# Graph kernel: opening with neighbour products by quarter of h

## The reference

```
h = relu(layernorm(x))
mask = adj > 0 ; deg = sum(mask, axis=1)
agg = mask @ h / max(deg, 1)
x = x + relu(concat(h @ W_self + b_self, agg @ W_nb + b_nb) @ W_comb + b_comb)

state = relu(layernorm(x))
5 times:
  s_in = state @ in_W.T + in_b ; s_out = state @ out_W.T + out_b
  a_in = adj @ s_in ; a_out = adj.T @ s_out
  r, z = sigmoid([a_in, a_out, state] @ (r_W, z_W).T + (r_b, z_b))
  h_hat = tanh([a_in, a_out, r * state] @ h_W.T + h_b)
  state = (1 - z) * state + z * h_hat
out = x + tanh(state @ o1_W.T + o1_b) @ o2_W.T + o2_b
```

## Time and profile before

| | |
|---|---|
| median of 3 runs | 1261.09 us |
| the profiled execution's own time | 1261.28 us |
| its span | 1259.5 us |
| TensorE busy | 1240.4 us, 98% |
| VectorE, ScalarE, GpSimd busy | 58%, 22%, 0% |
| chain of work that ended last | 88% TensorE |
| first instruction of TensorE | 6.21 us |
| first mask product (mean_sum(0)) | 40.19 us |
| first dense product | 61.16 us |
| mean granted TensorE clock, whole span | 0.995 |

### The profile page before, as it was taken

How to read it: one execution, slowest core, us unless ns; L and a number is a source line. 1 busy time by engine, 2 the same in 40 slices (tenths; PEclk the granted TensorE clock), 3 DMA queues, 4 the chain that set the end, 5 groups by cost and what they waited for, 6 DMA issues and landing times.

```text
span 1259.5 us, 12854 instructions
## 1 busy us (share of the span) xinstructions
PE 1240.4 (98%) x4922; PEld 603.4 (48%) x4922; DVE 725.3 (58%) x1222; ACT 279.8 (22%) x544; POOL 3.0 (0%) x9
## 2 busy tenths in 40 slices
PE   7999999999999999999999999999999999999998
PEld 5666654444444444444444444444444444444445
DVE  5577664055657468258547438845734963672674
ACT  4765311010104012022302103311211330120121
POOL 0000000000000000000000000000000000000000
PEclk9899999999999999999999999999999999999999
DMA  8354084006194920840480381074066019116201
GB/s 305 135 169 167 35 317 175 1 0 266 63 335 179 334 100 1 300 167 0 169 299 0 106 307 56 5 286 178 0 227 240 1 66 348 54 36 232 88 1 67
DMA packets 44410, 182.97 MB, mean 145 GB/s; under 512 B 3521, under 2 KB 13506, under 8 KB 28610
## 3 DMA queue, kind: packets, MB, share of 16 engines
q1 hardware_dynamic: 43344, 178.40, 38.9%
q0 software_dynamic: 720, 3.67, 0.8%
q10 hardware_dynamic: 290, 0.14, 0.0%
HBM read 147.07 MB, written 35.13 MB: 145 GB/s over the span
## 4 chain that ended last, share of the span: by engine, by line
PE 88%; DVE 1%; issue 0%; ACT 0%; DVEq 0%; ACTq 0%
PE bank L308 87%; PE bank L471 1%; PE bank L424 0%; DVE work L1203 0%; DVE ST L1205 0%; DVE H L1053 0%; DVE work L1201 0%; PE bank L377 0%; DVE DR L1021 0%; DVE work L1177 0%; DVE work L1181 0%; DVE AT L1010 0%; DVE LF L1148 0%; DVE res L1413 0%; DVE stat L960 0%
## 5 line engine op out<-in xcount | busy, mean ns | idle before, releaser
L308 PE MATMUL bank<-slot,LF 128*128 128x512 f16 x1792 | 389.4, 379 | 1.3 <-ACT m_buf L738 0.7
L308 PEld LDWEIGHTS bank<-slot,LF 128*128 128x128 f16 x1792 | 175.1, 98 | 212.7 <-issue 2.9
L308 PE MATMUL bank<-X,W 128*128 128x512 f32 x384 | 180.5, 593 | 0.0
L308 PE MATMUL bank<-XT,W 128*128 128x512 f32 x288 | 135.4, 593 | 0.0
L308 PEld LDWEIGHTS bank<-X,W 128*128 128x128 f32 x384 | 72.6, 190 | 87.9 <-issue 86.8
L308 PE MATMUL bank<-A,SN 128*128 (+1 forms) x256 | 97.2, 380 | 0.0
L308 PE MATMUL bank<-work,WG 128*128 128x512 f32 x224 | 97.1, 593 | 0.0
L308 PE MATMUL bank<-AT,SN 128*128 (+1 forms) x256 | 97.1, 379 | 0.0
L308 PEld LDWEIGHTS bank<-XT,W 128*128 128x128 f32 x288 | 54.8, 190 | 68.8 <-issue 68.1
L1224 DVE TENSOR_TENSOR u_buf<-bank,m_buf 128x512 f32<-128x512 f32 x16 | 11.1, 692 | 130.7 <-PE bank L308 130.7
L738 ACT ACTIVATE m_buf<-bank 128x512 f32<-128x512 f32 x40 | 23.8, 596 | 227.9 <-PE bank L308 227.9
(11 more groups left out here) (170 smaller groups left out, 1367.3 us busy)
## 6 DMA issues: line engine op xcount, KB each, us to landing
slot<-quad_d SPq DMA_DIRECT2D x112, 1024.0 KB, 5.6
WG<-in_adj SPq DMA_DIRECT2D x32, 512.0 KB, 4.3
quad_d<-AT SPq DMA_DIRECT2D x14, 1024.0 KB, 5.0
quad_d<-A SPq DMA_DIRECT2D x14, 1024.0 KB, 6.3
SN<-in_x SPq DMA_DIRECT2D x2, 1024.0 KB, 10.3
x_d<-SN POOLq DMA_DIRECT2D x4, 512.0 KB, 2.9
x1o<-x_d SPq DMA_DIRECT2D x1, 2048.0 KB, 8.2
out<-res SPq DMA_DIRECT2D x4, 512.0 KB, 3.0
```

The lines of the kernel that those rows point to most:

```text
L308: return pe.matmul(o, l, r, start=start, stop=stop, skip_group_check=again)
```

## The change

- By quarter: mean_sum(0) waits for quarter 0 of h only, and mean_sum(4), (8) and (12) for the others. On VectorE normal(0), normal(1) and low(0) stand ahead of the loop; low(1) to low(3) stand behind masks at i = 2, 5 and 9 (LOW_AT), normal(2) and normal(3) behind the first two of them. On ScalarE high(0) stands ahead of the loop, high(1) to high(3) at i = 1, 4 and 8 (HIGH_AT).
- The layernorm's factor is multiplied by SCALE once, so h32 holds scaled values without relu. The maximum with zero over each quarter goes; high is now an activation Relu, low takes max(h, 0) minus the high half in its one instruction, and the copies of transposed h apply relu and 1/SCALE.
- turn_h(0) to turn_h(3) move behind mean_sum(5), (7), (9) and (11) (TURN_AT), to banks 6 and 7; their copies stand four tiles later in the orders of ScalarE and VectorE.
- bias0's products and gcol's move behind mean_sum(1) (BIAS_AT). For gcol GpSimd first scales the gate weights by the bias columns (4 operations of 768 columns) and adds them in pairs (2), so that TensorE has 12 products with a column of ones.
- Ten products on zeros (WARM) stand ahead of TensorE's first work, and a small square root ahead of ScalarE's; both wait for two VectorE memsets.
- move_adj(0) goes ahead of the loop's first convert; W12's copies come behind high(0).

```diff
--- before.py
+++ after.py
@@ -37,6 +37,11 @@
 H2_AT = 12
+HIGH_AT = [1, 4, 8]
+LOW_AT = [2, 5, 9]
+TURN_AT = [5, 7, 9, 11]
+BIAS_AT = 1
+WARM = 10
 
@@ -117,6 +122,7 @@
         diag = work[:, 8192:16384].bitcast(FP16).rearrange("p (w t n) -> p w t n", w=2, t=NT)
+        idle16 = work[:, 0:2 * BN].bitcast(FP16)
         xs = SN[:, :, :, :].rearrange("p t s d -> p t (s d)").bitcast(FP32)
@@ -139,6 +145,8 @@
         h32 = AT[:, 1, :, :].rearrange("p t n -> p (t n)").bitcast(FP32).rearrange("p (t d) -> p t d", t=NT)
+        scaled = AT[:, 2, :, :].rearrange("p t n -> p (t n)").bitcast(FP32)[:, 0:4 * GATES].rearrange(
+            "p (w j n) -> p w j n", w=2, j=2)
         fusedS = AT[:, 3, :, :].rearrange("p t n -> p (t n)").bitcast(FP32)[:, 0:4 * GATES].rearrange(
@@ -158,6 +166,8 @@
         setup_done = sem("setup_done")
+        w12_sum, gsum, gcol_out = sem("w12_sum"), sem("gsum"), sem("gcol_out")
+        warm = sem("warm")
         var_ready, sqrt_ready = sem("var_ready"), sem("sqrt_ready")
@@ -294,6 +304,15 @@
         def _(pool):
+            pool.wait_ge(ld_c, 48)
+            for w in range(2):
+                pool.wait_ge(ld_w[w], 32)
+                for j in range(2):
+                    nc.gpsimd.tensor_scalar(scaled[:, w, j, :], wgR[w][:, j, :], col[:, 2 * w + j:2 * w + j + 1], None,
+                                            ALU.mult).then_inc(gsum, 1)
+                pool.wait_ge(gsum, 3 * w + 2)
+                nc.gpsimd.tensor_tensor(scaled[:, w, 0, :], scaled[:, w, 0, :], scaled[:, w, 1, :],
+                                        ALU.add).then_inc(gsum, 1)
             pool.wait_ge(fused_out, 8)
@@ -307,6 +326,10 @@
 
+
+            pe.wait_ge(warm, 2)
+            for e in range(WARM):
+                mm(bank[7][:, :], idle16[:, 0:P], idle16[:, :], True, True)
 
@@ -322,14 +345,14 @@
                 pe.wait_ge(h_ready, b + 1)
-                if b < 2:
-                    pe.wait_ge(fused_out, 2 * b + 6)
+                if b == 0:
+                    pe.wait_ge(gcol_out, 1)
                 else:
-                    pe.wait_ge(hT_act, b - 1)
-                    pe.wait_ge(hT_dve, b - 1)
+                    pe.wait_ge(hT_act, b)
+                    pe.wait_ge(hT_dve, b)
                 for f in range(FT):
                     for q in range(BT):
-                        last = pe.transpose(bank[4 + 2 * (b % 2) + f][:, q * P:q * P + P],
+                        last = pe.transpose(bank[6 + f][:, q * P:q * P + P],
                                             h32[:, BT * b + q, f * P:f * P + P], ident)
@@ -341,32 +364,27 @@
                                   wcR[:, 2 * w + j, :], j == 0, j == 1)
-
-            pe.wait_ge(left_ready, 1)
-            for j in range(4):
-                mm(bank[2][:, 0:D], L0[:, j, :], wcR[:, j, :], j == 0, False)
-            mm(bank[2][:, 0:D], cst[0:1, C_ONE:C_ONE + P], b_combR[0:1, :], False, True)
-            turn_h(0)
-            turn_h(1)
-
-            for w in range(2):
-                for t in range(6):
-                    for j in range(2):
-                        last = mm(bank[3][:, 6 * w + t:6 * w + t + 1], wgR[w][:, j, t * P:t * P + P],
-                                  col[:, 2 * w + j:2 * w + j + 1], j == 0, j == 1)
-            last.then_inc(setup_done, 1)
-            turn_h(2)
-            turn_h(3)
+            last.then_inc(w12_sum, 1)
+
+            def biases():
+                pe.wait_ge(left_ready, 1)
+                pe.wait_ge(fused_out, 8)
+                for j in range(4):
+                    mm(bank[7][:, 0:D], L0[:, j, :], wcR[:, j, :], j == 0, False)
+                mm(bank[7][:, 0:D], cst[0:1, C_ONE:C_ONE + P], b_combR[0:1, :], False, True)
+                pe.wait_ge(gsum, 6)
+                for w in range(2):
+                    for t in range(6):
+                        last = mm(bank[6][:, 6 * w + t:6 * w + t + 1], scaled[:, w, 0, t * P:t * P + P],
+                                  cst[:, C_ONE:C_ONE + 1], True, True)
+                last.then_inc(setup_done, 1)
 
...
                 pe.wait_ge(conv, 4 * (4 * b + m // 4 + 1))
-                if i == 2:
-                    pe.wait_ge(w12_out, 1)
                 if i == 0:
                     pe.wait_ge(id16_ready, 1)
-                    pe.wait_ge(hT_act, NB)
-                    pe.wait_ge(hT_dve, NB)
+                    pe.wait_ge(fused_out, 8)
                 if i >= 3:
@@ -380,9 +398,10 @@
                 pe.wait_ge(mask_ready, i + 1)
+                if m % BT == 0 and b == 0:
+                    pe.wait_ge(h_hi, m // BT + 1)
+                    pe.wait_ge(h_lo, m // BT + 1)
                 if m == 0 and b == 0:
-                    pe.wait_ge(h_hi, 4)
-                    pe.wait_ge(h_lo, 4)
                     pe.wait_ge(w12_out, 1)
@@ -402,6 +421,9 @@
                 pe.wait_ge(agg_dve, b + 1)
+                if b == 0:
+                    pe.wait_ge(hT_act, NB)
+                    pe.wait_ge(hT_dve, NB)
                 if b > 0:
@@ -428,6 +450,10 @@
                 mean_sum(i)
+                if i == BIAS_AT:
+                    biases()
+                if i in TURN_AT:
+                    turn_h(TURN_AT.index(i))
                 if i % NT == H2_AT and i > NT:
@@ -766,6 +792,8 @@
 
+            act.wait_ge(warm, 2)
+            nc.scalar.activation(nrm[:, 2, 0:1], nrm[:, 3, 0:1], ACT.Sqrt)
             for e in range(4):
@@ -776,22 +804,27 @@
                     convert(k, r)
-            for q in range(4):
+
+            def high(q):
                 act.wait_ge(h_ready, q + 1)
-                copy(hi_lo[:, BT * q:BT * q + BT, 0, :], h32[:, BT * q:BT * q + BT, :], SCALE).then_inc(h_hi, 1)
+                nc.scalar.activation(hi_lo[:, BT * q:BT * q + BT, 0, :], h32[:, BT * q:BT * q + BT, :],
+                                     ACT.Relu).then_inc(h_hi, 1)
+
             def move_h(q):
                 act.wait_ge(hT_ready, q + 1)
-                copy(ST[:, 0, q * BN:q * BN + BN], bank[4 + 2 * (q % 2)][:, :]).then_inc(hT_act, 1)
-
-            move_h(0)
-            move_h(1)
-            act.wait_ge(setup_done, 1)
+                nc.scalar.activation(ST[:, 0, q * BN:q * BN + BN], bank[6][:, :], ACT.Relu,
+                                     scale=1.0 / SCALE).then_inc(hT_act, 1)
+
+            def combined():
+                act.wait_ge(setup_done, 1)
+                copy(gcol[:, :, :].rearrange("p w t -> p (w t)"), bank[6][:, 0:12])
+                copy(bias0, bank[7][:, 0:D]).then_inc(gcol_out, 1)
+
+            high(0)
+            act.wait_ge(w12_sum, 1)
             for w in range(2):
-                copy(W12[:, 2 * w:2 * w + 2, :].rearrange("p k n -> p (k n)"), bank[w][:, :])
-            copy(gcol[:, :, :].rearrange("p w t -> p (w t)"), bank[3][:, 0:12])
-            copy(bias0, bank[2][:, 0:D]).then_inc(w12_out, 1)
-            move_h(2)
-            move_h(3)
+                ins = copy(W12[:, 2 * w:2 * w + 2, :].rearrange("p k n -> p (k n)"), bank[w][:, :])
+            ins.then_inc(w12_out, 1)
 
@@ -818,12 +851,20 @@
                 k = 2 * (i // 4 + 1) + i % 4 // 2
+                if i == 0:
+                    move_adj(0)
                 if k < 8 * NB:
...
                     block_end(i // NT - 1)[0]()
-                if i % 2 == 0:
+                if i % 2 == 0 and i:
                     move_adj(i)
+                if i in HIGH_AT:
+                    high(HIGH_AT.index(i) + 1)
+                if i - 4 == BIAS_AT:
+                    combined()
+                if i - 4 in TURN_AT:
+                    move_h(TURN_AT.index(i - 4))
                 if i >= NT and i % NT in STAGE_AT:
@@ -967,6 +1008,8 @@
 
+            v.memset(idle16, 0.0).then_inc(warm, 1)
+            v.memset(nrm[:, 3, 0:1], 1.0).then_inc(warm, 1)
             row_stats(range(NT), 0)
@@ -985,22 +1028,32 @@
                 link(v.reciprocal(rs, sc))
-
-            newton(NT, 1)
-            for q in range(4):
+                return rs
+
+            rs = newton(NT, 1)
+            link(v.tensor_scalar(rs, rs, SCALE, None, ALU.mult))
+
+            def normal(q):
                 for t in range(BT * q, BT * q + BT):
...
                                           ALU.subtract, ALU.mult)
-                link(ins)
-                hq = h32[:, BT * q:BT * q + BT, :].rearrange("p t d -> p (t d)")
-                v.tensor_scalar(hq, hq, 0.0, None, ALU.max).then_inc(h_ready, 1)
-            for q in range(4):
+                ins.then_inc(h_ready, 1)
+
+            def low(q):
+                dve.wait_ge(h_ready, q + 1)
                 dve.wait_ge(h_hi, q + 1)
                 v.scalar_tensor_tensor(out=hi_lo[:, BT * q:BT * q + BT, 1, :], in0=h32[:, BT * q:BT * q + BT, :],
-                                       scalar=SCALE, in1=hi_lo[:, BT * q:BT * q + BT, 0, :],
-                                       op0=ALU.mult, op1=ALU.subtract).then_inc(h_lo, 1)
```

(17 more changed lines are left out.)

## The result

The changed kernel took 1258.64 us (median of 20 runs, 1256.71 to 1261.6) against 1261.11 for the kernel before (median of 20, 1259.72 to 1261.62). The ratio is 0.9985, with a 95% interval of 0.9978 to 0.9991: 1.9 us less by the ratio, 2.5 by the medians, and between 1.1 and 2.8 by the interval. Forecast were 1257.9 and a change of 3.2.

A forecast was written before the change was run, and what follows sets the result against it. TensorE, busy 98% of 1259.5 us, was taken as the bound, with time to gain in its opening. 13.8 - 8.3 - 2.0 - 0.3 = 3.2 us less gave 1257.9; range 1256.0 to 1262.3.

The forecast's parts named there:

- T0: Start of TensorE's first neighbour (mask) product, mean_sum(0); 40.19 before the change, forecast 26.4.
- T0, removed: Opening: first mask product needs only quarter 0 of h, so it comes 13.8 us earlier, at 26.4.
- Idle products: TensorE's start: ten idle products bring the full clock sooner, 2.9 us off the fused products, not on T0's path.
- my sign of products 0.43 apart from 6.2 on: Expected in the profile after: TensorE's fused products at 0.43 intervals, full clock, from 6.2 on.
- Moved behind T0: TensorE: L0 and b_comb 2.15, bias columns 2.7, transposes of h 3.45; 8.3 us added.
- Stalls: First 16 tiles: TensorE waits 1.2 for mask(5) and 0.8 at turn_h(1); 2.0 us, bounds 0 and 8.5.
- Clock behind T0: TensorE's clock falls after little work from 21 to 26.4; +0.3 us, bounds -1.3 and +1.6.
- T1: Start of TensorE's first dense product, 61.16 before, forecast 57.9; what moves it moves the end.
- collision of the store: Rival: fused-weight store gets ahead of adjacency load 1, T0 at 29.1, 2.7 to 2.9 lost; 1260.8 us, chance 0.30.
- row of q0 alone: Queue row over 24 to 25: store's queue moves data alone though a load was issued; cited for the store rival.
- in-order stalls: Rival: VectorE's and ScalarE's in-order queues stall every insertion, stalls 8.5 not 2.0; 1264.2 us, slower, chance 0.11.
- Clock kept: Rival: TensorE's clock doesn't fall and stalls are hidden, 1.3 + 0.3 plus part of the stalls; 1256.0 us, chance 0.09.

The follow-up runs named there:

- All quarters ahead: Changed kernel with all four quarters of h (four normal, four low, four high) made before the adjacency loops; 1264.70 us, ratio 1.0030 to the kernel before.
- late table load: Changed kernel without the small square root ahead of ScalarE's fused copies, so the Sqrt table loads before the real square root; 1259.95 us (11 runs).

## Why the prediction was right, and what it missed

*T0, removed: 13.8 forecast, 14.1 found.* Newton at 20.30 (20.2 said), normal(0) at 21.70 (21.6), T0 at 26.11 (26.4). high(0) cost 1.06, as the copy did, and not 1.18, so the price that I gave the Relu's bias operand wasn't paid. All quarters ahead moved T0 by 5.5 and brought the median to 1264.70, above the kernel before: 5.5 of the 14.1 are the quartering, and without them the change loses. The rest is work of TensorE that moved behind T0, and Newton, which starts 1.3 earlier.

*Idle products: 2.9 off the fused products forecast, 1.0 found* in the changed kernel's trace (last fused copy at 18.73, before at 19.70), where my sign of products 0.43 apart from 6.2 on failed, and 2.7 to 2.9 in those of eight variants. Off T0's path, as said. GpSimd's six operations were sized wrong: 2.2 each for scaling and 1.8 for adding, 12.4 together. They ended at 19.1, just as the copies did, so the store was not delayed in this execution. In the seven traces in which the copies were done by 17.4 and GpSimd had this work, it was: issued at 18.8 to 19.0, against 17.69 with the bias sums on TensorE. For the bias columns there were 13 us to spare:

```profile
L311 POOL TENSOR_SCALAR AT<-A,col 128x768 f32<-128x768 f32 x4 | 8.8, 2200 | 6.2 <-DMA A<-in_wg_t 6.2
L314 POOL TENSOR_TENSOR AT<-AT 128x768 f32<-128x768 f32 x2 | 3.6, 1811 | 0.2
```

*Moved behind T0: 8.3 forecast, 8.9 found.* Biases took 5.62 (29.48 to 35.10), 0.4 of it the low clock; each of the four groups of transposes adds 0.91 (41.07 to 41.98) and not 0.86.

*Stalls: 2.0 forecast, 2.1 found*, at the two places named: 40.09 follows 38.66 by 1.43 where 0.22 is usual, and 45.23 follows 44.25 by 0.98 where 0.10 is.

*Clock behind T0: +0.3 forecast, +0.4 in the profiled execution* (3.4 low, half of it lost, less the 1.3 of before). With these, 14.1 - 8.9 - 2.1 - 0.4 gives 2.7, and T1 moved 2.74. That this term came out is in part luck: the profiled execution had one fall of 3.4 us, and the six variants with an unbroken run of columns had low stretches of 3.4 to 13.7 us in all.

*What was missed* is in the clock term: I bounded it by one fall behind T0. A run of 24 one-column passes is followed by a further one in some executions and not in others. The row of the kernel before that should have told me is the same one from which I took the price of a pass: the clock had fallen within its 48. Of the seven traces with an unbroken run (the changed kernel and six variants) six have a second or late fall, four within the run (1.8 to 3.8 us into it) and two 1.0 and 1.3 us behind its end, low for 3.4 to 6.8 us; with the run broken up none of four has one there, and nothing above 1259.2 was timed. The median of 20 came out 0.7 above the forecast only in part for that reason: without the seven executions above 1260 it would be 1258.36. I also took 0.2 off from the profiled execution to the median, as in the kernel before; here the profiled one lies 0.35 below it. That the second fall explains the times near 1261.5 of the changed kernel itself is argued from clocks, not seen in a trace of those executions.

*Rivals.* The collision of the store didn't happen, not even with the store issued at 17.69, where by my account it would have stood in front of load 1. The row of q0 alone over 24 to 25 shows a load waiting that was issued after the store, not before it, so it says nothing of loads already queued; and as that load had waited since 22.86, it speaks against taking turns, not for it as I had it. By the rule that I cited from the Trainium skill ("DMA: Bandwidth & Descriptors", Queues, rings and completion order), that an engine takes its queues in turn by packet, either could have gone first and the two would have taken turns; the traces don't show that. What was issued first went first: the three loads before the store, and in the changed kernel's trace the store before the loads issued at 20.71 and 22.0, with q0 alone moving data over 22 to 24 (68 packets, 0.84 MB). The in-order stalls were as walked and no more (that rival's time should have read 1264.4, 6.5 above the forecast). "Clock kept" came by itself at T0 in one trace of eight (the late table load's), not in the changed kernel's; filling the wait kept it in three of three, worth 1.5 in the medians of the same rounds (1256.33 to 1254.83) once the further fall was out of the way.

## What to carry to other kernels

Treat a thin stretch of TensorE like an idle one when you sum up the clock: a wait of 3 us, or a run of 24 one-column fp32 passes, each cost 1.7 to 3.4 us (half of a low stretch of 3.4 to 6.8) in executions that were hit. Break such runs up between full products, and fill a wait on the way to them with products nobody reads if their end is sure to come before the wait's. And where times of one kernel lie in groups, compare mean clocks before medians: 0.6 us of an edit can't be read in medians that hang on which group was drawn.

## What the runs showed of the hardware

- TensorE's clock came up at different times in executions that began with equal work: between 9.2 and 9.9 in the changed kernel's trace, and within the ten idle products in others (they took 4.45 us in the changed kernel's, 3.71 in the late table load's; at the low clock 0.43 each). In the kernel before it came up at about 12.0. The windows read 1.00 in all of this time.
- Low stretches lasted from 3.4 to 10.2 us. Two lasted 10.2: one in the kernel before, from 4.5 us into its 48 one-column passes, and one with all quarters ahead, which began in 8.9 us of idle time before T0.
- A GpSimd operation on 768 fp32 columns took 2.2 us for one input with a column of factors and 1.8 for two inputs, against 0.34 for a VectorE one of 256 columns.
- An activation Relu of 1024 columns took 1.06 us, as the copy, and needed no table load behind Sqrt.
- A store issued by GpSimd at 17.69, behind three queued loads, moved its first data 3.1 us later; in the kernel before, issued at 20.39, it took 1.2 us, its first data at 21.6 behind the last of the loads at 21.25. Loads issued behind the store moved nothing until it was through.
